# Attention masks made by GpSimd ahead of use instead of by DVE between its logits

## The reference, cut to what matters

```
att = where(edge_adj > 0, e_plus[None, :], NEG_INF)
att = where(edge_adj < 0, e_minus[None, :], att)
att = softmax(att, axis=1)
out = att * edge_adj @ hW          # summed over 3 heads, divided by 3
```

## Time and profile before

| | us |
|---|---|
| median of 3 runs | 914.15 (908.91 to 914.3) |
| the profiled execution | 913.46 |
| its span in the trace | 911.7 |
| TensorE busy | 811.1 (89%) |
| DVE busy | 686.8 (75%) |
| ACT busy | 514.8 (56%) |
| GpSimd busy | 233.7 (26%) |

### The profile page before, as it was taken

The page is one execution under the profiler, slowest core; times in us unless marked ns, Lnnn a source line. Parts: engine busy times, 40 slices in busy tenths (PEclk is TensorE's granted clock), DMA queues, the critical chain, the costliest instruction groups (busy, mean ns, idle before and its releaser), DMA issues. The chain is left out here.

```text
span 911.7 us, 11859 instructions
## 1 busy us (share of the span) xinstructions
PE 811.1 (89%) x4180; PEld 516.8 (57%) x4180; DVE 686.8 (75%) x988; ACT 514.8 (56%) x818; POOL 233.7 (26%) x135
## 2 busy tenths in 40 slices
PE   6999988999999999999789989989959979887565
PEld 6655537888888888874345559984323222331211
DVE  3986889999999999607942227864088899899997
ACT  2754537777777777634520127523557577676661
POOL 4000000000000000000000020001298889889993
PEclk8999998999999999999989989999879999997876
DMA  8689986220221121039410000000331713526410
GB/s 285 208 315 336 344 290 253 93 93 0 92 92 40 52 92 46 1 133 422 185 28 0 1 1 1 1 1 23 73 104 40 171 46 99 126 53 155 105 47 12
DMA packets 38960, 101.67 MB, mean 112 GB/s; under 512 B 6113, under 2 KB 11114, under 8 KB 32386
## 3 DMA queue, kind: packets, MB, share of 16 engines
q1 hardware_dynamic: 38354, 100.83, 33.6%
q10 hardware_dynamic: 560, 0.27, 0.1%
HBM read 75.60 MB, written 18.14 MB: 103 GB/s over the span
## 5 line engine op out<-in xcount | busy, mean ns | idle before, releaser
L1871 PE MATMUL PS<-big 128*128 128x256 f32 x768 | 194.6, 385 | 3.4 <-ACT big L1701 3.3
L221 PE MATMUL PS<-ident,big 128*128 128x128 f32 x1123 | 158.7, 281 | 29.0 <-DVE big L1398 8.1
L221 PEld LDWEIGHTS PS<-ident,big 128*128 128x128 f32 x1123 | 137.4, 146 | 52.8 <-issue 20.9
L470 POOL TENSOR_TENSOR big<-big 128x1024 f32<-128x1024 f32 x64 | 149.7, 2358 | 10.6 <-DVE big L1437 9.9
L1871 PEld LDWEIGHTS PS<-big 128*128 128x128 f32 x768 | 133.7, 191 | 21.7 <-ACT big L1701 7.1
L1701 ACT ACTIVATE big<-PS 128x512 f32<-128x512 f32 x192 | 105.1, 599 | 58.6 <-PE PS L221 57.7
L431 POOL MEMSET big<- 128x16 f32 x1 | 0.1, 131 | 520.5 <-PE PS L835 520.5
L1437 DVE TENSOR_TENSOR_SCAN big<-PS,stripes,big 128x512 f32<-128x512 f32 x96 | 116.7, 1263 | 5.8 <-ACT PS L734 3.8
L2070 DVE SCALAR_TENSOR_TENSOR big<-big,rz 128x2048 f32<-128x2048 f32 x48 | 112.7, 2350 | 0.9
L2048 DVE CUSTOM_DVE_ANT_0 big<-big 128x2048 f32<-128x2048 bf16 x48 | 109.7, 2289 | 0.1
L734 ACT ACTIVATE PS<-big,stripes 128x512 f32<-128x512 f32 x128 | 86.1, 685 | 33.8 <-DVE big L1437 33.2
(11 more groups left out here) (211 smaller groups left out, 973.9 us busy)
## 6 DMA issues: line engine op xcount, KB each, us to landing
big<-in_adj SPq DMA_DIRECT2D x16, 2048.0 KB, 9.3
big<-at_dram SPq DMA_DIRECT2D x4, 4096.0 KB, 28.0
at_dram<-big SPq DMA_DIRECT2D x3, 4096.0 KB, 17.0
big<-b_dram SPq DMA_DIRECT2D x32, 256.0 KB, 4.3
big<-big SPq DMA_DIRECT2D x24, 256.0 KB, 4.0
big<-b_dram SPq DMA_DIRECT2D x36, 128.0 KB, 4.0
at_dram<-big SPq DMA_DIRECT2D x1, 3072.0 KB, 18.6
big<-e_dram SPq DMA_DIRECT2D x3, 1024.0 KB, 6.3
```

The costliest lines, as they stand in the source:

```text
L221: return nc.tensor.transpose(PS[:, bank, col:col + P], src, ident[:])
L470: nc.gpsimd.tensor_tensor(dbu[k % 3], du2[c % 2][:, 2 * (n % 2):2 * (n % 2) + 2, :], bb[group % 2][:, pair_of(k) % 2, :].unsqueeze(1).to_b ...
L1871: m = nc.tensor.matmul(PS[:, 4 + k // 3, 0:256], hw[:, jt, h, :], qt[v % 4][:, 256 * c:256 * c + 256], start=(h == 0 and jt == 0), stop=(h ...
```

## The change

GpSimd gets a function `edge_mask` of its own, with the same two instructions, for row tiles 2 to 15. It is called 14 times in a straight line between the first constants and `later_pool`. GpSimd waits for the landing of the tile (`a2_in`), for its own product (`offd_done`) and, where a buffer of `bm` is used again, for the logits that read it last (`x_done`). Before the first it waits for DVE's two own masks, for the flags of the scores (`flag_seen`) and for the rows of scores to be written out (`e_out`). `later_pool`, with its constants, stands behind all 14. In DVE's logits, the call of `edge_mask` gives way to a wait for `bm_done`. DVE's own `edge_mask` remains for tiles 0 and 1.

```diff
@@ -1610,6 +1610,28 @@
             pool.wait_ge(comb_ready, 17)
             nc.gpsimd.tensor_copy(comb_e0, comb[:, 1:2].to_broadcast([P, P])).then_inc(comb_ready, 1)
+
+            def edge_mask(it, pair, j, reused):
+
+                tile = it * 4 + 2 * pair + j
+                pool.wait_ge(a2_in[pair], it * 16 + 16)
+                blk = aw[pair][:, j, tile * P:(tile + 1) * P]
+                nc.gpsimd.tensor_tensor(blk, blk, dgt[:], ALU.mult).then_inc(offd_done, 1)
+                pool.wait_ge(offd_done, tile + 1)
+                if reused:
+                    pool.wait_ge(x_done, it * 12 + 6 * pair + j - 7)
+                nc.gpsimd.tensor_scalar(bm[2 * pair + j], aw[pair][:, j, :], 0.0, MASKED, ALU.is_le,
+                                        ALU.mult).then_inc(bm_done, 1)
+
+            pool.wait_ge(bm_done, 2)
+            pool.wait_ge(flag_seen, NCH)
+            pool.wait_ge(e_out, 16 * NCH)
+            for j in range(2):
+                edge_mask(0, 1, j, False)
+            for it in range(1, NT // 4):
+                for pair in range(2):
+                    for j in range(2):
+                        edge_mask(it, pair, j, True)
             later_pool(pool)
@@ -2031,7 +2053,7 @@
                     pair, h = k // 3 % 2, k % 3
                     s = 2 * h + j
                     if h == 0 and k:
-                        edge_mask(it, k, j)
+                        dve.wait_ge(bm_done, it * 4 + 2 * (k // 3) + j + 1)
                     if h == 0:
                         dve.wait_ge(eb0_ready, 1)
                         dve.wait_ge(e1_done, NT)
```

## The result

The changed kernel takes 947.63 us (median of 4 runs, 944.4 to 952.21) against 912.97 for the kernel before on the same chip: a ratio of 1.039, with a 95% interval of 1.036 to 1.043. It is slower, by three times what was forecast, and lies above the stated range, which ended at 944. The span of its profiled execution is 946.5 us, 34.8 more than before. Nothing outside the attention moved: TensorE's first transposes of the attention begin at 140.39 us (140.31 before), and those that follow it, 34.55 us later than before, at 436.39 (401.84).

The account below looks back on a forecast made before the run. The prediction took TensorE to bound the attention, with DVE close behind. Its terms, -5.1 + 13.4 + 2 + 1.5 = +11.8 us on the profiled 913.46, gave 925 us, with a range of 908 to 944.

Parts of the forecast that it names:

- TensorE sets the pace, at most 5.1 us to gain: Attention loop: TensorE is the bound, so removing DVE's masks returns only its seven long steps, -5.1 us.
- The two engines hold each other: Attention: a GpSimd instruction fully holds DVE's logits and weights, which read two SBUF tiles; 3.8 us a pair.
- The mask costs 2.1 us: GpSimd's 128x2048 mask, priced from one-input selects at 0.95 ns an element: 2.1 us, with 4.5 kept for the range.
- Rival 2: Hold with a dear mask on GpSimd, 3 to 4.5 us: 940 us at 3.2, 959 at 4.5; chance 17%.
- Six pairs, +13.4: Later pairs of row tiles: holds make the second exponential 2.45 us late, taken as 2.2 a pair, +13.4 us.
- First pair +2: Tiles 2 and 3 at the loop's start: a product and part of two masks delay it, +2 us (0.46 to 5.1).
- Setup +1.5: GpSimd's setup for a later stage, now behind the last mask under the attention: +1.5 us, between 0 and 3.4.
- Masks ready in time: Between a tile's landing and DVE's use, both masks fit, so DVE's new wait for them costs nothing by itself.

Follow-up runs that it names:

- x2: The changed kernel with GpSimd filling the mask buffers with zeros, no masks and no diagonal product (masking of tiles 2 to 15 left out): 908.06 us, ratio 0.997.
- x3: The kernel before, all masks on DVE, each pair's first mask made one step earlier and the second where the first was: 909.59 us, ratio 0.997.
- x9: The changed kernel with GpSimd's mask replaced by a multiply and an add of the same size (masking of tiles 2 to 15 left out): 917.11 us, ratio 1.004.
- x1: The kernel before with a bench behind its end, GpSimd instructions alone, then beside DVE operations: the mask alone takes 7.08 us; whole time means nothing.
- x8: The kernel before with a second bench of GpSimd forms alone and beside DVE: multiply and maximum 7.09 us, maximum alone 5.37; whole time means nothing.
- x11: The changed kernel with each of GpSimd's 14 masks in three pieces (640, 704 and 704 columns): 921.37 us, ratio 1.011.
- x13: The changed kernel with each of GpSimd's masks in two instructions of 1024 columns: 935.93 us, ratio 1.025.
- x7: The changed kernel with the masks of tiles 2 and 3 on DVE again, GpSimd making those of tiles 4 to 15: 941.53 us, ratio 1.031.
- x6: The changed kernel with GpSimd's setup for the last layer back at the start, ahead of the masks: 945.91 us, ratio 1.037.

## Why the prediction was wrong

- *TensorE sets the pace, at most 5.1 us to gain*: right as far as it can be resolved. The attention of x2 and x3 is 5.2 and 4.4 us shorter in their traces; the medians give 3.5 and 2.0.
- *The two engines hold each other*: right, and with it the sign. x2 against x9 shows that it is what GpSimd reads; x1 and x8 show that DVE operations with two SBUF inputs are held and reductions with one are not. The rule of the Trainium skill (SBUF — State Buffer, "Who interferes with whom") says the same of who is held; its "for the whole instruction" holds here only for GpSimd's wait and for the DVE tensor_scalar, not for two-input operations, which come free after 4.3 of 7.08 us.
- *The mask costs 2.1 us* is the step that failed. It costs 7.08, above the end of 4.5 that I kept for the range and above the estimate of 1.8 to 3.5 that I had worked out from the Trainium skill, and bars DVE for 4.3. I took the price from a select, whose row says nothing of a comparison in a tensor_scalar. Rival 2 had the mechanism; its hold of 3 to 4.5 us is what came, and I gave it 17% and 940 to 959 us. That its times fit is in part luck: it took the hold to be as long as the mask, and set both at 3 to 4.5. x9 shows it: the same number of instructions over the same elements with a price of 1.90 give +3.4 us (1.0037) in place of +34.7. x11 and x13 show that it is the hold and not GpSimd's time by itself: there GpSimd's masks take no less time in sum (127.6 and 132.5 us against 114.5), the holds fall from 58 us to 15 and 13, and the loss that is left comes with DVE's waits for masks.
- *Six pairs, +13.4*: 5.05 us a pair (36.8 less 32.5, and the 0.73 given back), +30.3. With the price forecast it would have been too high, though: by x9 0.2 us a pair net of the gain, where I had 1.5, and 917 where I had 925. So the step from holds to TensorE's time was mis-sized as well, the other way. The two holds of a pair are 0.4 to 0.9 and 1.7 us there; what takes them up, the four PSUM banks or the lead of the weights, no run separates.
- *First pair +2*: 5.2 us net, so 5.9; x7 gives 5.6 back by its steps. It lies above both of my bounds (0.46 and 5.1), since two operations of DVE are held for 4.03 and 4.27 us there; and I chose low between them, in the one place without any lead.
- *Setup +1.5*: 3.2 us, near the upper bound of 3.4. The last pair takes 40.0 us where the others take 36.8, and in x6 the two long steps in it are gone; x6's time does not resolve it. Sum of the steps: -5.1 + 30.3 + 5.9 + 3.2 = +34.3, of the 34.55 us by which the attention ends later.
- *Masks ready in time*: right for the changed kernel, in which DVE never stood at its wait for a mask. From the second turn on, the first mask of a pair is ready 10.9 us ahead of the logits that read it, the second at least 4.2; tile 3's has 1.9 (160.84 to 162.78). It was closer than I said: x11 and x13, whose shorter instructions make a pair's masks later and whose DVE gets there sooner, have such waits.

## What to carry to other kernels

Work moved to GpSimd is only taken from DVE as far as GpSimd doesn't hold DVE meanwhile. In this kernel what counted was how long GpSimd's reads bar DVE's two-input operations, set against what DVE spent on the work itself (4.3 against 1.5 us). Price the very form of the instruction, with its pair of operations, before moving it. And look first at whether the owner can do it in a stall of its own: a move by one step in DVE's order (x3) brought 4.4 of the 5.2 us that the traces show there was to gain.

## What the runs showed of the hardware

- GpSimd's tensor_scalar over 128x2048 depends on the operations: multiply and add 1.90 us, cast 1.89, fill 1.80; is_le or maximum alone 5.37; is_le, is_gt or maximum in a pair with multiply 7.08 to 7.09. The output's type made no difference (7.08 into bfloat16 and into float32).
- A GpSimd instruction that reads SBUF bars a two-input DVE operation for a part of its length. For is_le and multiply that is 0.9 ns a column up to 1024 columns, and 3.9 and 4.3 us at 1536 and 2048, where multiply and maximum has 4.4. Multiply and add over 2048 columns bars for 1.75 of its 1.90 us (x9, from 174.10), a two-input product of 1024 for 2.2 of 2.34. Why the hold ends where it does isn't shown. Reading in blocks of 1024, the second after the arithmetic of the first (3.5 us at 3.46 ns), would give 4.0 and 4.4 for the two long ones. That fits the five sizes of the mask within 0.2 us, but it is a reading of them.
- A DVE tensor_scalar from SBUF to SBUF is held nearly to the end of GpSimd's instruction, not only of its reads; reductions with one input are not held; fills by GpSimd hold no two-input operation.
